# Attention and gated feed-forward on one core: value products by two query tiles, and the maxima of two heads in one VectorE instruction

## The chip, the core and the metric

The kernel runs on one core of a Trainium2 chip. The core has a matmul engine (TensorE, PE in the profile), three elementwise engines (VectorE or DVE, ScalarE or ACT, GpSimd or POOL), and SyncE (SP), which here issues the DMAs. The engines have their own instruction streams and wait for each other with semaphores. The metric is the device time of one execution in microseconds; the median of the runs is compared.

## The reference

Two layers act on x of 4 x 512 x 512. Each adds to x an attention of the normalised x, multiplied by a gate that a feed-forward network makes of the same normalised x. The change touches layer 0 only:

```
xn   = layernorm(x)
q    = xn @ Wq   (32 heads of 16);   k, v = xn @ Wk, xn @ Wv   (8 heads of 16, each shared by 4 query heads)
p    = softmax(q k^T / 4)            (512 x 512 for each head and batch)
s    = concat(p v) @ Wo
g    = silu(down(fwht(silu(gate(fwht(xn))) * up(fwht(xn)))))   (512 -> 2048 -> 512, fwht is a Walsh-Hadamard transform)
x    = x + s * g
```

Layer 1 (a delta-rule attention over six heads and a feed-forward network with sign weights) follows. It is not touched.

## The kernel before, in words

Layer 0's work is written out by hand as a list of steps t from 0 to 295. Every engine runs its own loop over t and, in each step, does whatever is due at that t. Nothing is planned at run time: an engine's instructions go in the order of its loop, and semaphores make it wait for the others.

A unit u is one batch with one key head and its four query heads: 32 units of 8 steps, so a batch is 64 steps. In a unit, two steps belong to one query tile of 128 rows; these two are called a double step here. In it:

- `scores` (TensorE, even step): four matmuls of 32 x 128 by 32 x 512, one for each of the four heads, side by side in the array, into four PSUM banks (the first two banks are the tensor `vpair`). It waits until the four exponentials of the tile before are done, since these read the same banks.
- `row_max` (VectorE, even step): four reduces of 128 x 512, one for each head, negated.
- `exps` (ScalarE): the exponentials of heads 0 and 1 in the even step, of heads 2 and 3 in the odd one, written as fp16 to one of three slots of `probs`.
- `turn_probs` (SP, next even step): a DMA transpose of the four heads' probabilities to a quarter of the columns of `probsT`. From the second unit on it waits for the value products of the unit before (L344).
- `weigh` (TensorE, third step of the next unit): the value products of the whole unit, 16 matmuls of 128 x 32 by 128 x 512 over four column tiles, into the bank `OB`. It stands behind the scores of that step and waits for all four transposes.
- `to_tokens`, `divide`, `to_features` (VectorE, some of the divisions on POOL): a transpose of `OB`, the division by the sum of the exponentials, and the transpose back, at steps 3, 4 and 6 of the next unit.
- `load_heads` (SP, step 6): eight small DMAs that spread k and q of the unit after the next over the partitions.

Beside the attention run the feed-forward products. In the last 32 steps of a batch (m from 32 on) TensorE does a gate tile in the even step and an up tile in the odd one, eight matmuls of 512 columns each (`ffn_mm`), into two banks in turn. ScalarE makes tanh of the gate tile (`tanh_gate`, odd step, ahead of the exponentials), VectorE multiplies (`gate_mul`, `up_mul`), ScalarE copies the result to fp16 (`high_rows`, at the end of the even step, between the two pairs of exponentials), POOL or VectorE makes the rest (`low_rows`). A matmul into a bank waits until the tile two before has been taken from it. In the first 32 steps of the next batch (m below 32) TensorE does the down products, six matmuls in each step (`down_mm`). I call these stretches gate stage and down stage. In the first batch the first 32 steps hold instead the Hadamard transform of the up and gate weights: POOL's and VectorE's sums, fp32 matmuls (`transform_ug`), and copies by ScalarE (`high_half`, after the exponentials) and VectorE (`low_half`). From step 49 the down weights are transformed likewise. The projections of q, k and v of later units lie at steps 5 of every 16, and 43 and 49 of the batch; their evictions by ScalarE follow one step later. The output projection lies in steps 17, 19, 28 and 35.

In TensorE's loop of a step the order is: scores, value products, transposes of x, weight transforms, sums, and then the feed-forward products.

## Time and profile before

| | us |
|---|---|
| median of 3 runs | 1487.92 (1484.96 to 1489.2) |
| profiled execution | 1479.72 |
| its span, first to last instruction | 1477.9 |
| TensorE busy | 1278.4 (87%) |
| VectorE busy | 1058.7 (72%) |
| ScalarE busy | 775.1 (52%) |
| POOL busy | 524.5 (35%) |
| mean granted TensorE clock | 0.963 |

The shares are means over the whole span. Layer 0's steps end at about 840 us and the rest is layer 1, where TensorE is busy nearly all the time; in layer 0 it is not. Busy time of TensorE counts matmuls with their whole pipeline, whose ends are modelled. The granted clock is 1.0 at 2.4 GHz.

### The profile page before, as it was taken

The page shows a single profiled execution, that of the slowest core. Times are in us where ns is not written, and L with a number is a line of the kernel's source. Part 1 is how long each engine was busy: PE and PEld are TensorE (multiplying, and loading weights), DVE is VectorE, ACT ScalarE, POOL GpSimd, SP SyncE. Part 2 cuts the span into 40 slices and gives each one's busy share as a digit, 9 for nine tenths or more (in the row PEclk, how much of TensorE's full clock was granted, in tenths as well). Part 3 has the DMA queues.
Part 4 walks back from the last instruction along what each step waited for, and adds up shares of the span by engine and source line. Part 5 has one row for each costly group of instructions (what it writes and reads, how often), then busy time and mean ns, then how long its engine had stood idle before and what let it go on. Part 6 is the DMA issues. An engine that isn't in the chain of part 4 may idle for free. (4 is left out here: it accounts for less than half of the span.)

```text
span 1477.9 us, 22423 instructions
## 1 busy us (share of the span) xinstructions
PE 1278.4 (87%) x8226; PEld 640.0 (43%) x8226; DVE 1058.7 (72%) x1823; ACT 775.1 (52%) x1308; POOL 524.5 (35%) x434
## 2 busy tenths in 40 slices
PE   4777788777877787877888899999999999999998
PEld 2232333232322233322333355585548654765466
DVE  6688877666766567656777498687878688669846
ACT  5676666554655557545661775236533554246532
POOL 2389853002210022100221156323733274317531
PEclk9899999998999999999999999999999999999999
DMA  7775545565555665565657502300230111210221
GB/s 242 187 168 99 92 91 90 105 123 104 92 104 98 130 114 98 106 119 114 112 102 227 212 20 55 86 16 29 55 71 23 37 45 43 55 37 19 55 48 44
DMA packets 346557, 135.52 MB, mean 92 GB/s; under 512 B 312176, under 2 KB 333392, under 8 KB 343888
## 3 DMA queue, kind: packets, MB, share of 16 engines
q1 hardware_dynamic: 334032, 132.52, 40.6%
q10 hardware_dynamic: 12416, 1.57, 1.0%
q8 instruction: 66, 1.08, 0.3%
q14 instruction: 43, 0.35, 0.1%
HBM read 44.87 MB, written 17.87 MB: 42 GB/s over the span
## 5 line engine op out<-in xcount | busy, mean ns | idle before, releaser
L929 ACT ACTIVATE probs<-vpair,top_n 128x512 f16<-128x512 f32 x256 | 164.4, 687 | 256.3 <-DVE top_n L627 256.3
L1143 PE MATMUL bank<-rows,both 128*128 128x512 f16 x1024 | 244.7, 392 | 5.2 <-DVE fd L700 4.1
L627 DVE TENSOR_REDUCE top_n<-vpair 128x1 f32<-128x512 f32 x256 | 164.5, 684 | 84.9 <-PE bank L1114 82.8
L443 POOL TENSOR_TENSOR h<-th,h 128x512 f16<-128x512 f32 x61 | 71.5, 1172 | 271.5 <-ACT h L898 271.5
L627 DVE TENSOR_REDUCE top_n<-bank 128x1 f32<-128x512 f32 x256 | 163.7, 681 | 0.0
L929 ACT ACTIVATE probs<-bank,top_n 128x512 f16<-128x512 f32 x256 | 162.6, 690 | 0.0
L1143 PEld LDWEIGHTS bank<-rows,both 128*128 128x128 f16 x1024 | 97.5, 100 | 144.5 <-issue 35.4
L2218 PE MATMUL bank<-rows,both 128*128 128x512 f16 x512 | 118.3, 382 | 0.0
L1114 PE MATMUL vpair<-qk 32*128 32x512 f16 x256 | 50.4, 389 | 74.4 <-ACT probs L929 74.4
L2234 PE MATMUL bank<-both,hid 128*128 128x512 f16 x512 | 111.2, 379 | 0.0
L1128 PE MATMUL bank<-probsT,vaug 128*32 128x512 f16 x512 | 45.3, 487 | 72.3 <-DMA probsT<-probs 60.4
L1157 PE MATMUL bank<-dn,h 128*128 128x512 f16 x256 | 104.1, 407 | 0.9 <-DVE tg L633 0.9
L2202 PE MATMUL bank<-rows,both 128*128 128x512 f16 (+1 forms) x456 | 104.0, 379 | 0.9 <-PEq L159 0.9
L1158 PE MATMUL bank<-dn,h 128*128 128x512 f16 x256 | 103.1, 403 | 0.0
L1159 PE MATMUL bank<-dn,h 128*128 128x512 f16 x256 | 102.4, 400 | 0.0
L633 DVE SCALAR_TENSOR_TENSOR tg<-tg,bank 128x512 f32<-128x512 f32 x64 | 44.0, 687 | 72.3 <-ACT tg L941 71.8
L456 POOL TENSOR_TENSOR otok<-oblk,rl 128x256 f16<-128x256 f32 x25 | 15.5, 620 | 180.0 <-DVE rl L673 180.0
L2234 PEld LDWEIGHTS bank<-both,hid 128*128 128x128 f16 x512 | 50.1, 98 | 60.4
L2218 PEld LDWEIGHTS bank<-rows,both 128*128 128x128 f16 x512 | 48.4, 100 | 55.4 <-issue 0.8
L1114 PEld LDWEIGHTS vpair<-qk 32*128 32x128 f16 x256 | 12.9, 91 | 131.3 <-ACT probs L929 74.2
L2202 PEld LDWEIGHTS bank<-rows,both 128*128 128x128 f16 (+1 forms) x456 | 43.6, 98 | 55.5 <-issue 4.4
L1593 POOL TENSOR_TENSOR big<-big,both 128x384 f32<-128x384 f32 x32 | 32.0, 1026 | 94.5 <-DMA big<-t_scratch 70.3
(362 smaller groups left out, 2673.3 us busy)
## 6 DMA issues: line engine op xcount, KB each, us to landing
h<-in_ug SPq DMA_DIRECT2D x8, 1024.0 KB, 5.8
lt_scratch<-big SPq DMA_DIRECT2D x16, 384.0 KB, 2.7
dn<-in_down SPq DMA_DIRECT2D x2, 2048.0 KB, 11.1
x_scratch<-th SPq DMA_DIRECT2D x16, 256.0 KB, 2.6
res<-x_scratch SPq DMA_DIRECT2D x16, 256.0 KB, 4.1
out_x<-res SPq DMA_DIRECT2D x16, 256.0 KB, 2.0
both<-in_w SPq DMA_DIRECT2D x2, 1548.0 KB, 11.9
t_scratch<-tok SPq DMA_DIRECT2D x16, 192.0 KB, 2.1
```

The costliest lines, as they stand in the source:

```text
L443: pool.tensor_tensor(h16(ft, 1), row32, h16(ft, 0), ALU.subtract).then_inc(S["row_lo"], 1)
L627: v.tensor_reduce(top_n[:, i:i + 1], SC_[n % G][:, :], AX.X, ALU.max, negate=True).then_inc(S["max_done"], 1)
L929: a.activation(probs[:, k % TAKEN, j * T:(j + 1) * T], SC_[j][:, :], ACT.Exp, bias=top_n[:, i:i + 1]).then_inc(S["p_ready"], 1)
L1114: pe.matmul(SC_[j][:, :], qs[32 * j:32 * j + 32, u % SLOTS, qt * P:(qt + 1) * P], ks[32 * j:32 * j + 32, u % SLOTS, :], start=True, stop=T ...
L1128: mm = pe.matmul(OB[32 * j:32 * j + 32, :], vaug[:, b % 2, kt, g, :], probsT[:, TT * j + kt, :], start=kt == 0, stop=kt == TT - 1)
L1143: mm = pe.matmul(GB[n % 2][:, :], w[:, kt, col:col + P], xnb(b, kt), start=r == 0, stop=r == 2 * KT - 1)
L1157: pe.matmul(bk, h16(ft, 0)[:, rows], dn16(ft, 0), start=j == 0, stop=False)
L1158: pe.matmul(bk, h16(ft, 0)[:, rows], dn16(ft, 1), start=False, stop=False)
L1159: mm = pe.matmul(bk, h16(ft, 1)[:, rows], dn16(ft, 0), start=False, stop=j == FT - 1)
L2202: mm = pe.matmul(bk, lhs(i, kt), rhs(j, kt), start=n == 0, stop=n == 3 * KT - 1)
L2218: mm = pe.matmul(fbank[ht % 2][:, :], up[:, kt, ht * P:(ht + 1) * P], x_half(i, kt), start=kt == 0 and i == 0, stop=kt == KT - 1 and i == 1)
L2234: mm = pe.matmul(fbank[tt % 2][:, :], hid[:, i, ht, tt * P:(tt + 1) * P], down[:, ht, :], start=ht == 0 and i == 0, stop=ht == HT - 1 and ...
```

## The change

The value products of a unit are made in two halves of two query tiles each (256 columns), two double steps after the last exponentials that they need; a transpose waits only for the half product that read its place. Token transposes, divisions and feature transposes move to later steps. The maxima of heads 0 and 1 come from one reduce over both banks of `vpair`; those of heads 2 and 3 stay single. TensorE does some feed-forward matmuls of a double step (four or three of the gate tile, one or none of the down products) ahead of the scores, and transposes of x and the weight transforms too. ScalarE copies `high_rows` and `high_half` ahead of the step's exponentials. The head loads are split into k (step 6) and q (step 2 of the unit before), and the evictions of q, k and v come two steps after their projection from step 70 on. Semaphore counts of `pv_done` double everywhere.

```diff
@@ -32,7 +32,9 @@
 BSTEPS = NKV * STEPS
 SLOTS = 4
 TAKEN = 3
-PV_STEP, TOKEN_STEP, DIVIDE_STEP, TURN_BACK = 2, 3, 4, 6
+TOKEN_STEP, DIVIDE_STEP, TURN_BACK = 4, 6, 2
+GATE_AHEAD, DOWN_AHEAD = (4, 3), (1, 0)
+LATE_EVICT = 70
 OT = KT + 1
 FFN_STEP = 32
 DOWN_END = (8, 16, 24, 32)
...
@@ -307,7 +309,13 @@
                     sp.wait_ge(S["s_ps"], (u - SLOTS + 1) * SC)
                 for j in range(G):
                     sp.dma_start(ks[32 * j:32 * j + DH, slot, :], kst[DH * g:DH * g + DH, :]).then_inc(S[f"heads_in{slot}"], 16)
+
+            def load_q(u):
+
+                slot = u % SLOTS
                 sp.wait_ge(S["mb_took"], MB["q", u // 2] + 1)
+                if u >= SLOTS:
+                    sp.wait_ge(S["s_ps"], (u - SLOTS + 1) * SC)
                 for j in range(G):
                     r = 64 * (u % 2) + DH * j
                     sp.dma_start(qs[32 * j:32 * j + DH, slot, :], qst[r:r + DH, u // 2 % 2, :]).then_inc(S[f"heads_in{slot}"], 16)
...
@@ -341,11 +349,12 @@
                 u, qt = divmod(n, TT)
                 sp.wait_ge(S["p_ready"], G * (n + 1))
                 if u:
-                    sp.wait_ge(S["pv_done"], u)
+                    sp.wait_ge(S["pv_done"], n // 2 - 1)
                 sp.dma_start_transpose(probsT[:, :, qt * P:(qt + 1) * P], probs[:, n % TAKEN, :]).then_inc(S[f"pt_in{n % TAKEN}"], 16)
 
-            load_heads(0)
-            load_heads(1)
+            for u in range(2):
+                load_k(u)
+                load_q(u)
             sp.dma_start(wsd[:, :], d["wscale_dp"].partition_broadcast(P)).then_inc(S["wo_in"], 16)
             for t in range(TEND):
                 b, m = t // BSTEPS - 1, t % BSTEPS
@@ -362,8 +371,10 @@
                     sp.dma_start(wo[:, :, :], d["wo"]).then_inc(S["wo_in"], 16)
                 if (t - PREP - 2) % 4 == 0 and 2 <= (t - PREP - 2) // 4 + 2 < NCH:
                     load_chunk((t - PREP - 2) // 4 + 2)
-                if t % STEPS == STEPS - 2 and 1 < t // STEPS + 2 < NU:
-                    load_heads(t // STEPS + 2)
+                if t % STEPS == 6 and t // STEPS + 2 < NU:
+                    load_k(t // STEPS + 2)
+                if t % STEPS == 2 and 1 < t // STEPS + 1 < NU:
+                    load_q(t // STEPS + 1)
                 if b >= 0 and m in XRES_STEP:
                     tt = XRES_STEP.index(m)
                     n = b * TT + tt
...
@@ -620,6 +631,12 @@
             def half_scale():
                 v.tensor_scalar(top[:, 4:5], powr[:, 0:1], 0.5 * float(D) ** -0.5 / SUM_RAISE, None, ALU.mult).then_inc(S["pow_b"], 1)
 
+            def two_maxima(n):
+
+                v.wait_ge(S["s_ps"], n + 2)
+                i = n % (2 * SC)
+                v.tensor_reduce(top_n[:, i:i + 2], W["vpair"][:, :, :], AX.X, ALU.max, negate=True).then_inc(S["max_done"], 2)
+
             def row_max(n):
 
                 v.wait_ge(S["s_ps"], n + 1)
...
@@ -659,7 +676,7 @@
 
             def to_tokens(u):
 
-                v.wait_ge(S["pv_done"], u + 1)
+                v.wait_ge(S["pv_done"], 2 * (u + 1))
                 if u:
                     v.wait_ge(S["o_done"], u)
                 v.transpose(oblk[:, :, :].rearrange("p c d -> p (c d)"), OB[:, :]).then_inc(S["o_free"], 1)
@@ -790,8 +807,9 @@
                 if t > FFN_STEP + 1 and (t - 2) // BSTEPS < B and (t - 2) % BSTEPS >= FFN_STEP and t % 2 == 0:
                     up_mul((t - 2) // BSTEPS, ((t - 2) % BSTEPS - FFN_STEP) // 2)
                 if t < NU * STEPS and t % 2 == 0:
-                    for j in range(G):
-                        row_max(2 * t + j)
+                    two_maxima(2 * t)
+                    row_max(2 * t + 2)
+                    row_max(2 * t + 3)
                 if t == 1:
                     statistics(3)
                 if t == 2:
@@ -812,8 +830,8 @@
                     to_tokens(t // STEPS - 1)
                 if t % STEPS == DIVIDE_STEP and 0 <= t // STEPS - 1 < NU:
                     divide(t // STEPS - 1)
-                if t % STEPS == TURN_BACK and 0 <= t // STEPS - 1 < NU and t // STEPS % 2 == 0:
-                    to_features(t // STEPS - 1)
+                if t % STEPS == TURN_BACK and 0 <= t // STEPS - 2 < NU and t // STEPS % 2:
+                    to_features(t // STEPS - 2)
                 if b == B and m == 3:
                     next_stats()
                     weight_max(0)
...
@@ -980,28 +998,29 @@
                     deviations(3)
                 if t == 3:
                     normalise(3)
+                if t > FFN_STEP + 1 and (t - 2) // BSTEPS < B and (t - 2) % BSTEPS >= FFN_STEP and t % 2 == 0:
+                    high_rows((t - 2) // BSTEPS, ((t - 2) % BSTEPS - FFN_STEP) // 2)
                 if b < B and m > FFN_STEP and m % 2:
                     tanh_gate(b, (m - FFN_STEP) // 2)
+                if 0 <= t - PREP - 2 < NCH * KT:
+                    high_half(t - PREP - 2)
                 if t < NU * STEPS:
                     exps(2 * t)
                     exps(2 * t + 1)
                 if t in TURN_STEP:
                     evict_x(KT + TURN_STEP.index(t))
-                if 0 <= t - PREP - 2 < NCH * KT:
-                    high_half(t - PREP - 2)
                 for ft in range(FT):
                     if ABS_AT[ft] == t:
                         magnitudes(ft)
                 if t in DN_AT:
                     high_down(DN_AT.index(t))
-                if t % 16 == Q_STEP + 1 and t // 16 + 1 < NU // 2:
+                late = 1 if t < LATE_EVICT else 2
+                if t % 16 == Q_STEP + late and t // 16 + 1 < NU // 2:
                     evict_q(t // 16 + 1)
-                if m == V_STEP + 1 and b + 1 < B:
+                if m == V_STEP + late and b + 1 < B:
                     evict_v(b + 1)
-                if m == K_STEP + 1 and b + 1 < B:
+                if m == K_STEP + late and b + 1 < B:
                     evict_k(b + 1)
-                if t > FFN_STEP + 1 and (t - 2) // BSTEPS < B and (t - 2) % BSTEPS >= FFN_STEP and t % 2 == 0:
-                    high_rows((t - 2) // BSTEPS, ((t - 2) % BSTEPS - FFN_STEP) // 2)
                 if b and m - 1 in DOWN_END:
                     tanh_down((b - 1) * TT + DOWN_END.index(m - 1))
                 if b == B and m == 9:
@@ -1114,18 +1133,20 @@
                     pe.matmul(SC_[j][:, :], qs[32 * j:32 * j + 32, u % SLOTS, qt * P:(qt + 1) * P],
                               ks[32 * j:32 * j + 32, u % SLOTS, :], start=True, stop=True).then_inc(S["s_ps"], 1)
 
-            def weigh(u):
-
+            def weigh(n):
+
+                u, half = divmod(n, 2)
                 b, g = divmod(u, NKV)
-                for i in range(TAKEN):
-                    pe.wait_ge(S[f"pt_in{i}"], 16 * ((TT * (u + 1) - 1 - i) // TAKEN + 1))
-                if u:
+                for k in (2 * n, 2 * n + 1):
+                    pe.wait_ge(S[f"pt_in{k % TAKEN}"], 16 * (k // TAKEN + 1))
+                if u and half == 0:
                     pe.wait_ge(S["o_free"], u)
-                if g == 0:
+                if g == 0 and half == 0:
                     pe.wait_ge(S["mb_took"], MB["v", b] + 1)
+                cols = slice(2 * P * half, 2 * P * (half + 1))
                 for kt in range(TT):
                     for j in range(G):
-                        mm = pe.matmul(OB[32 * j:32 * j + 32, :], vaug[:, b % 2, kt, g, :], probsT[:, TT * j + kt, :],
+                        mm = pe.matmul(OB[32 * j:32 * j + 32, cols], vaug[:, b % 2, kt, g, :], probsT[:, TT * j + kt, cols],
                                        start=kt == 0, stop=kt == TT - 1)
                 mm.then_inc(S["pv_done"], 1)
 
...
@@ -1144,21 +1165,29 @@
                 if r == 2 * KT - 1:
                     mm.then_inc(S["gb_full"], 1)
 
-            def down_mm(n, j):
+            def down_mm(n, j, r):
 
                 k, ft = GO["down", n], DN_TURN[j]
-                if j == 0:
+                if j == 0 and r == 0:
                     pe.wait_ge(S["gb_took"], k - 1)
-                if n % TT == 0:
+                if n % TT == 0 and r == 0:
                     pe.wait_ge(S["row_lo"], n // TT * FT + ft + 1)
-                if n == 0:
+                if n == 0 and r == 0:
                     pe.wait_ge(S["mb_took"], MB["dn", j] + 1)
                 bk, rows = GB[k % 2][:, :], slice(n % TT * P, (n % TT + 1) * P)
-                pe.matmul(bk, h16(ft, 0)[:, rows], dn16(ft, 0), start=j == 0, stop=False)
-                pe.matmul(bk, h16(ft, 0)[:, rows], dn16(ft, 1), start=False, stop=False)
-                mm = pe.matmul(bk, h16(ft, 1)[:, rows], dn16(ft, 0), start=False, stop=j == FT - 1)
-                if j == FT - 1:
+                mm = pe.matmul(bk, h16(ft, r // 2)[:, rows], dn16(ft, r % 2), start=j == 0 and r == 0, stop=j == FT - 1 and r == 2)
+                if j == FT - 1 and r == 2:
                     mm.then_inc(S["gb_full"], 1)
+
+            def ffn(t, first, last):
+
+                b, m = t // BSTEPS, t % BSTEPS
+                if b and m < FFN_STEP:
+                    for i in range(first, min(last, 6)):
+                        down_mm((b - 1) * TT + m // 8, 2 * (m % 8) + i // 3, i % 3)
+                if b < B and m >= FFN_STEP:
+                    for r in range(first, last):
+                        ffn_mm(b, m - FFN_STEP, r)
 
             def turn_next():
                 pe.wait_ge(S["p_ready"], NU * SC)
@@ -1194,24 +1223,23 @@
             sum_maxima(0)
             for t in range(TEND):
                 b, m = t // BSTEPS, t % BSTEPS
-                if t < NU * STEPS and t % 2 == 0:
-                    scores(t // 2)
-                if t % STEPS == PV_STEP and 0 <= t // STEPS - 1 < NU:
-                    weigh(t // STEPS - 1)
                 if t in TURN_STEP:
                     turn_x(KT + TURN_STEP.index(t))
                 if 0 <= t - PREP - 2 < NCH * KT:
                     transform_ug(t - PREP - 2)
+                ahead = 0
+                if t % 2 == 0:
+                    ahead = (DOWN_AHEAD if m < FFN_STEP else GATE_AHEAD)[t // 2 % 2]
+                ffn(t, 0, ahead)
+                if t < NU * STEPS and t % 2 == 0:
+                    scores(t // 2)
+                if t % 4 == 0 and 0 <= t // 4 - 2 < 2 * NU:
+                    weigh(t // 4 - 2)
+                ffn(t, ahead, 2 * KT)
                 if t > 0 and t % 4 == (PREP + 1) % 4 and (t - PREP) // 4 < NCH:
                     sum_maxima((t - PREP) // 4)
                 if t in DN_AT:
                     transform_dn(DN_AT.index(t))
-                for half in range(2):
-                    if b and m < FFN_STEP:
-                        down_mm((b - 1) * TT + m // 8, 2 * (m % 8) + half)
-                    if b < B and m >= FFN_STEP:
-                        for r in range(KT * half, KT * half + KT):
-                            ffn_mm(b, m - FFN_STEP, r)
                 if t % 16 == Q_STEP and t // 16 + 1 < NU // 2:
                     project_q(t // 16 + 1)
                 if m == V_STEP and b + 1 < B:
```

## Rows read from the trace of the kernel before

**Rows 1.** Busy time by stretch; then TensorE's granted clock, DMA share, GB/s.
```profile
21.44:242.90 221.46, 170.18 (x747) 67.37 (x747) 171.20 (x283) 152.26 (x261) 147.93 (x112) 0.95 0.60 130
242.90:777.48 534.58, 417.92 (x2233) 160.88 (x2233) 354.11 (x575) 302.78 (x505) 82.56 (x82) 0.93 0.59 108
242.90:327.95 85.05, 67.67 (x350) 25.36 (x349) 53.42 (x88) 45.20 (x74) 7.00 (x8) 0.92 0.62 117
427.19:513.53 86.34, 64.11 (x341) 23.88 (x341) 50.21 (x84) 42.86 (x70) 7.01 (x8) 0.90 0.59 116
605.47:690.20 84.73, 63.81 (x340) 23.87 (x341) 50.22 (x84) 42.86 (x70) 7.01 (x8) 0.92 0.63 118
88.00:170.00 82.00, 61.80 (x272) 24.02 (x273) 70.17 (x117) 53.27 (x95) 78.71 (x62) 0.96 0.60 119
461.00:472.00 11.00, 9.72 (x52) 4.00 (x52) 8.21 (x14) 7.32 (x12) 0.62 (x1) 1.00 0.56 106
```

**Rows 2.** Timeline of a double step in a gate stage: start, length, engine, line.
```profile
422.36 0.39 PE L1114 MATMUL vpair<-qk 32*128 32x512 f16 x2 [1.04 <-ACT probs L929]
...
422.69 3.63 PE L1143 MATMUL bank<-rows,both 128*128 128x512 f16 x16
422.78 1.29 DVE L627 TENSOR_REDUCE top_n<-vpair 128x1 f32<-128x512 f32 x2
423.51 1.29 ACT L929 ACTIVATE probs<-vpair,top_n 128x512 f16<-128x512 f32 x2 [1.20 <-DVE top_n L627]
...
424.69 0.62 ACT L898 ACTIVATE h<-th 128x512 f16<-128x512 f32 x1
425.21 0.68 ACT L941 ACTIVATE tg<-bank,usc 128x512 f32<-128x512 f32 x1
...
425.78 1.26 ACT L929 ACTIVATE probs<-bank,top_n 128x512 f16<-128x512 f32 x2
425.92 0.69 DVE L633 SCALAR_TENSOR_TENSOR tg<-tg,bank 128x512 f32<-128x512 f32 x1 [0.65 <-ACT tg L941]
...
427.19 0.39 PE L1114 MATMUL vpair<-qk 32*128 32x512 f16 x2 [0.87 <-ACT probs L929]
```

**Rows 3.** Timeline of a double step in a down stage; last, one single reduce.
```profile
461.05 0.39 PE L1114 MATMUL vpair<-qk 32*128 32x512 f16 x2
...
461.47 1.29 DVE L627 TENSOR_REDUCE top_n<-vpair 128x1 f32<-128x512 f32 x2 [3.50 <-PE bank L1114]
...
464.74 0.39 PE L1114 MATMUL vpair<-qk 32*128 32x512 f16 x2 [0.59 <-ACT probs L929]
...
L627 DVE TENSOR_REDUCE top_n<-vpair 128x1 f32<-128x512 f32 x256 | 164.5, 684 | 84.9 <-PE bank L1114 82.8
```

**Rows 4.** Timeline at value products in a gate stage.
```profile
410.90 1.05 PE L1128 MATMUL bank<-probsT,vaug 128*32 128x512 f16 x16 [1.57 <-DMA probsT<-probs]
...
411.88 5.28 PE L1143 MATMUL bank<-rows,both 128*128 128x512 f16 x16
```

**Rows 5.** Timeline at value products in a down stage, with SP's issues.
```profile
466.59 2.99 SPq L309 DMA_DIRECT2D qk<-kst  x4
...
467.08 1.29 ACT L929 ACTIVATE probs<-bank,top_n 128x512 f16<-128x512 f32 x2
...
469.63 2.48 SPq L313 DMA_DIRECT2D qk<-qst  x4
...
472.21 1.80 SPq L345 DMA_TRANSPOSE probsT<-probs  x1
...
476.81 1.90 PE L1128 MATMUL bank<-probsT,vaug 128*32 128x512 f16 x16 [4.02 <-DMA probsT<-probs]
```

**Rows 6.** Line 1128, the value products: what ended TensorE's idle time before them.
```profile
  DMA probsT<-probs: 91.2, 31
```

**Rows 7.** Lines 345 (transpose, landing) and 561 (a reduce of 2048 elements, ns).
```profile
DMA to landing us min/median/max: 4.3/4.3/10.7
...
L561 DVE TENSOR_REDUCE amax<-h x7: 2252/2274/2277, 33.3 to 120.3; 128x1 f32<-128x2048 f32 x7
```

**Rows 8.** Timeline, first gate stage: VectorE waits for POOL.
```profile
147.64 0.75 DVE L646 SCALAR_TENSOR_TENSOR th<-bank,hsc,tg 128x512 f32<-128x512 f32 x1 [3.29 <-POOL hsc L429]
```

More of the change, by code:

```diff
@@ L298, in _, with load_k @@
             load_chunk(1)
-            def load_heads(u):
+            def load_k(u):
                 b, g, slot = u // NKV, u % NKV, u % SLOTS
@@ L330, in load_raw @@
                 if i == 0:
-                    sp.wait_ge(S["pv_done"], NU)
+                    sp.wait_ge(S["pv_done"], 2 * NU)
                 if i == 2:
@@ L917, in evict_v @@
                 if b >= 2:
-                    a.wait_ge(S["pv_done"], (b - 1) * NKV)
+                    a.wait_ge(S["pv_done"], 2 * (b - 1) * NKV)
                 a.activation(vaug[:, b % 2, :, :, 0:DH], MISC[:, :].rearrange("p (t g c) -> p t g c", t=TT, g=NKV),
```

## Prediction

> **What bounds the kernel now.** I read the stretches first. Layer 0's attention runs from 21.44 to 777.48 us, 128 double steps of one query tile each; the rest, 700.4 us of the span, the diff hardly touches. The first batch's stage takes 221.46 us for 32 double steps, the three stages with down products 85.05, 86.34 and 84.73 (16 double steps each), and the three with up and gate products what is left of 534.58, that is 278.5 for 47 intervals [rows 1]. No engine is full in them: TensorE is busy 64 of 86 us, ScalarE 43, VectorE 50. So a ring of waits sets the pace, and the timeline shows it. In a gate stage: scores at 422.36, first maximum 0.42 later, first exponential at 423.51, two exponentials until the row copy at 424.69, tanh at 425.21, the last two exponentials from 425.78 to 427.04, next scores at 427.19. Round trip 4.83; TensorE's 16 products of 3.63 lie inside, with idle time behind them [rows 2]. In a down stage it is 3.69 [rows 3].
>
> Once in four double steps the value products break this ring. In the gate stage they wait 1.57 us for a transpose, and the 16 products behind them then take 5.28 instead of 3.63, at half clock (1.2 of 2.4 GHz: their pitch doubles) [rows 2, 4]. In the down stage it is worse. The exponentials of the last tile end at 468.4, but SP is still issuing the head loads (2.99 + 2.48 us), its transpose goes out only at 472.21 and TensorE's wait of 4.02 ends at 476.81, 8.4 after the data was ready [rows 5]. The matmul's own line sums 91.2 us of TensorE idle for this DMA, 31 times [rows 6].
>
> **The change, part by part**, against the profiled execution's 1479.72 us (span 1477.9 and 1.8 around it).
>
> *Value products by two query tiles, later.* The last transpose a half needs is issued after its own double step, and the product stands behind two further rounds: 2 x 4.2 = 8.4 us at the least, against 4.3 from issue to landing [rows 7]. That covers landing even with one head load (3.0) ahead of it on SP. I take the wait as gone, and with it the half clock behind it. The matmuls double in number and halve in columns: two groups of 16 in place of one that holds TensorE for 0.98 [rows 4]. Each new group costs between 0.5 (half the columns) and 0.98 (as before); I take 0.8. In a down double step TensorE then has 0.33 for the scores, 0.8, and 12 products at a pitch of 0.216 ((3.63 - 0.39) / 15, [rows 2]), 3.7, in a gate one, with 16, 4.6, both below the rings computed next, so it costs nothing; without that cover it would be 0.6 per unit, 19 us.
>
> *One maximum over two banks.* One 128x512 reduce lasts 0.68, one of 2048 elements 2.27 [rows 3, 7]: 1.04 ns an element, so 1024 take 1.22 (at most 1.29, the pair's time). VectorE saves 0.07, but the first exponential now waits 1.22 instead of 0.68: +0.54 on the ring in every double step. This is the change's price. On the pair, the second reduce is already issued before the first ends (1.29 for two, 0.68 for one), so little start cost is exposed. The Trainium skill (Advanced Engine Details and Errata, TRN2 Errata) says the memory latency shows as a bubble between instructions and recommends reading several PSUM banks at once. By that rule merging would save VectorE more; the sum would not move, since VectorE does not bind here.
>
> *The down ring.* 3.69 + 0.54 = 4.23. Nothing else of the change lies in it (the products put ahead of the scores run while TensorE would wait for exponentials). 48 x 4.23 = 203, plus 4 for double steps in which the output projection (1.03) meets value products: 207 against 256.1, so -49.
>
> *The gate ring.* The row copy (0.52 from start to start) moves ahead of the exponentials, into the time in which ScalarE waits for the maximum: it leaves the ring. But three or four gate products now stand ahead of the scores, and the bank of each gate needs the previous gate's multiply on VectorE. Counted from the scores: maximum 0.42 to 1.64, exponential at 1.69, tanh 1.18 later at 2.87, ends 3.55, multiply 3.58 to 4.27, 0.12 of semaphore, then 4 or 3 products at 0.216: scores again at 5.25 or 5.04, mean 5.14 [rows 2]. The exponentials alone would allow 3.44 + 1.26 + 0.15 = 4.85, so the wait for the multiply takes the place of the wait for exponentials. 47 x 5.14 = 242, plus 3 for projections: 245 against 278.5, so -34.
>
> *Token transposes and division, one or two steps later; transpose of features in the next unit.* Same instructions. The token transpose (0.7) now falls between the last maximum (2.9) and the multiply (3.58), which it just fits; if it doesn't, 0.1 per unit, 3 us at most. Lost cover: nothing waits for it within two rounds.
>
> *Head loads split, late q, k and v evictions.* SP issues the same eight loads of a unit, at most 3.0 us in one block rather than 5.5 [rows 5]. The evictions move off the middle of the ring to behind it; that frees about 0.5 sixteen times, inside the totals above. load_q gains a wait on scores that are over by then; behind it on SP stands the next transpose, and behind that the exponentials three tiles on and the value products two rounds on, so a microsecond here reaches nobody. The k eviction of a next batch now comes one step after the last q load it waits for (2.5 on SP and its landing); ScalarE stands still for at most 2 us, three times, behind exponentials that are already done.
>
> *First batch.* POOL is busy 78.7 of 82 us between 88 and 170, with weight transforms that gate what follows [rows 1], and up_mul waits 3.29 for it [rows 8]. So at most 3 there. In the other 139 us I take 9%, under the gate stage's 12% because the fp32 transforms add TensorE and VectorE work: 12. Bounds of the term 0 and 25; I take 15. Moving the weight-transform copy ahead of the exponentials hides it in the wait for the maximum there, which about pays the 0.54.
>
> *Tail.* The last value products lose a 2 us wait; 1.
>
> Sum: 49 + 34 + 15 + 1 = 99. Rings worked out from single rows come out short; the next down round after the 3.69 is 3.77 already (464.74 to 468.51, 0.14 after the exponentials that end in rows 5). I add 0.1 to each of the 95 double steps for it, 9.5. That leaves -90: 1390 profiled. The runs of before have median 1487.92, 8.2 above their profiled one; I carry the difference over: 1398.
>
> **Rivals.**
> A. The multiply isn't late, and the gate ring is 4.85: 47 x 0.29 = 14 less, 1384. For it: each step in 5.14 is a minimum-slack sum, and one overlap would shorten it. Against: bank order is fixed by the code. 0.15.
> B. SP becomes the bound of the down stages. Its work in a unit is 4 transposes at 1.8 and 5.5 of loads [rows 5], 12.7 of 17 us. If an issue took half as long again because the DMA queues are fuller, and the residual's transfers, one or two of a microsecond, came on top, it would be 18 to 19. 12 units x 2 us: 1422. Against: at 4.2 us apart transposes are further from each other than their issue. 0.14.
> C. Half the gate gain and all of the first batch's are eaten by POOL and by products that meet in one double step: 1398 + 17 + 15 = 1430. 0.13.
> D. The clock falls: slower. TensorE would idle 0.4 to 1.2 us in every double step (5.14 or 4.23 less its 3 to 4.6 of work), without end. At half clock a gate double step needs 16 x 0.43 (twice the pitch) + 0.7 = 7.6 instead of 5.14 and a down one 12 x 0.43 + 0.7 = 5.9 instead of 4.23: about 2 us each. If all 95 ran so: 190, 1588; from 45 of them on it is slower than before. Against: between stalls the present ring has the same gaps (0.59 to 1.04) and the granted clock of a stretch with three of them is 1.00 [rows 1 to 3]. The Trainium skill (TensorE: Matmul & The Clock Gate, on a second failure mode) warns of just this, many short idles between groups making the clock oscillate; by that rule this rival would be the case, and the trace so far does not agree. 0.04.
> E. The value products still wait, because a transpose now waits for the product two halves back and the two drift together. Then only the half clock goes: 28 x 1.65 = 46 less, against 48 x 0.54 and 47 x 0.31 more on the rings: 5 less, 1483, within what can be told. 0.04.
> My forecast: 0.50, for itself 1384 to 1412.
>
> **Numbers.** Predicted 1398. The range 1374 to 1432 takes in A, B and C and the term bounds of the first batch (+15, -10) and of the maximum (1.29: +0.07 x 95 = 7). A measurement tells 0.3%, 4.5 us. Faster: forecast, A, B, C and the milder half of E and D, 0.93; same: 0.04; slower: D at its full price, 0.03.
>
> **What would show it.** The value products' idle for the transpose (91.2) falls under 10; the maximum over two banks lasts 1.22; down double steps 4.2, gate ones 5.0 and 5.25 in turn, with TensorE's idle ahead of the gate products put down to the multiply (tg), not to the exponentials; granted clock 1.00 in all six stages; stages of about 70 and 82 us. I am wrong if down double steps exceed 4.6, if the transposes go out later than 1 us after their exponentials, or if half-clock stretches remain.

## The result and the profile after

The changed kernel takes 1432.32 us (median of 4) against 1486.66 for the kernel before: ratio 0.9637, 95% interval 0.9616 to 0.9657. It is 54 us faster; I had said 90 (1398), and the time lies just above the range's upper end, 1432. The profiled execution's span went from 1477.9 to 1430.6.

These are the stretches from one stage's first scores to the next, in the columns of [rows 1]: the start; the first 32 steps; the whole first batch, which contains them; then down and gate stages in turn; the tail.

```profile
0.00:25.39 25.39, 11.84 (x47) 5.57 (x49) 16.17 (x46) 10.33 (x19) 7.52 (x12) 1.00 0.64 213
25.39:160.64 135.25, 92.19 (x359) 35.17 (x360) 90.42 (x142) 85.14 (x145) 86.76 (x62) 0.86 0.64 148
25.39:262.89 237.50, 176.58 (x857) 68.20 (x857) 166.84 (x247) 151.51 (x256) 147.07 (x112) 0.91 0.57 121
...
262.89:338.93 76.04, 62.72 (x417) 25.32 (x417) 52.69 (x73) 44.93 (x75) 6.50 (x8) 1.00 0.72 131
338.93:424.39 85.46, 72.93 (x477) 29.08 (x478) 67.65 (x93) 59.66 (x100) 21.54 (x21) 1.00 0.64 112
424.39:494.94 70.55, 58.95 (x408) 23.96 (x408) 48.78 (x68) 41.94 (x70) 6.50 (x8) 1.00 0.78 142
494.94:580.41 85.47, 72.94 (x477) 29.06 (x478) 67.66 (x93) 59.66 (x100) 21.54 (x21) 1.00 0.64 112
580.41:650.95 70.54, 58.95 (x407) 23.96 (x408) 48.77 (x68) 41.94 (x70) 6.50 (x8) 1.00 0.79 142
650.95:731.49 80.54, 66.82 (x435) 25.91 (x435) 63.83 (x87) 54.78 (x91) 19.77 (x19) 1.00 0.63 110
731.49:1430.60 699.11, 680.63 (x5220) 406.51 (x5219) 516.78 (x922) 313.80 (x530) 287.97 (x229) 0.99 0.23 62
```

Beside [rows 1]: the down stages fell from 256.1 to 217.1 us, the three gate stages from 278.5 to 251.5, and all six now run at clock 1.00 (0.92, 0.90 and 0.92 in the down stages before). The first batch rose from 221.5 to 237.5, and it starts 4 us later; the whole rise lies in its first 32 steps, which in the kernel before took 117.5 us:

```profile
21.44:138.90 117.46, 85.56 (x311) 34.39 (x311) 89.62 (x155) 86.78 (x150) 76.31 (x49) 0.93 0.70 169
```
So 66 us were gained in the six stages, 20 were lost before them, and 1 was gained in the tail.

The value products' wait is gone. The idle time before the line, all of it, was 91.2 us for the DMA [rows 6] and 68.2 of "issue" (the engine waited for nothing that the profile shows); now it is 15.3 of "issue" alone:

```profile
L1149 PE MATMUL bank<-probsT,vaug x1024: 272/273/421, 58.8 to 742.4; 128*32 128x256 f16 x171
its engine sat idle before it (us, times) until:
  issue: 15.3, 64
```

Next a double step of a gate stage, as in [rows 2]: the 12 or 13 products behind the scores, the merged maximum, tanh, the multiply (DVE L650), three products of the next tile ahead of the scores, the next scores.

```profile
403.77 0.39 PE L1133 MATMUL vpair<-qk 32*128 32x512 f16 x2
...
404.09 0.62 PE L1149 MATMUL bank<-probsT,vaug 128*32 128x256 f16 x16
...
404.30 1.23 DVE L638 TENSOR_REDUCE top_n<-vpair 128x2 f32<-128x1024 f32 x1 [0.77 <-PE bank L1133]
404.65 2.76 PE L1164 MATMUL bank<-rows,both 128*128 128x512 f16 x12
405.44 1.28 DVE L644 TENSOR_REDUCE top_n<-bank 128x1 f32<-128x512 f32 x2
405.56 1.27 ACT L947 ACTIVATE probs<-vpair,top_n 128x512 f16<-128x512 f32 x2 [1.36 <-DVE top_n L638]
406.71 0.69 ACT L959 ACTIVATE tg<-bank,usc 128x512 f32<-128x512 f32 x1
407.28 1.27 ACT L947 ACTIVATE probs<-bank,top_n 128x512 f16<-128x512 f32 x2
407.43 0.69 DVE L650 SCALAR_TENSOR_TENSOR tg<-tg,bank 128x512 f32<-128x512 f32 x1 [0.71 <-ACT tg L959]
...
408.18 0.82 PE L1164 MATMUL bank<-rows,both 128*128 128x512 f16 x3 [0.76 <-DVE tg L650]
408.93 0.39 PE L1133 MATMUL vpair<-qk 32*128 32x512 f16 x2
```

The ring of the prediction can be followed step by step: the maximum lasts 1.23, the multiply is over at 408.12, the products that waited for it (`<-DVE tg`) start at 408.18, and the scores at 408.93, 5.16 after the last ones. The first exponential comes 1.79 after the scores; in the kernel before it was 1.15 [rows 2]. The exponentials were over at 408.55, so they no longer set the pace.

In the first 32 steps TensorE transposes x (L1053) ahead of the weight transform (L1074) and the scores (L1133), and a transpose can wait for ScalarE's eviction (L879) of the one before. Here ScalarE ends step 17 and TensorE begins step 18:

```profile
100.86 1.27 ACT L947 ACTIVATE probs<-bank,top_n 128x512 f16<-128x512 f32 x2
...
102.00 0.62 ACT L879 ACTIVATE rows<-bank 128x512 f16<-128x512 f16 x1
...
102.77 0.38 PE L1053 MATMUL bank<-ident,both 128*128 128x128 f16 x4 [2.89 <-ACT rows L879]
102.99 1.08 PE L1074 MATMUL bank<-h,had 128*128 128x512 f32 x2
...
104.86 0.39 PE L1133 MATMUL vpair<-qk 32*128 32x512 f16 x2
104.96 0.69 ACT L897 ACTIVATE both<-bank,suc 128x512 f16<-128x512 f32 x1 [1.82 <-PE bank L1075]
```

The exponentials end at 102.13. Scores that waited for them alone could have come at about 102.25 (an estimate: 0.12 for the semaphore, as in the prediction). They come at 104.86, since an eviction, a transpose and a transform stand in between.

### The profile page after: what moved, and what is told of

It is laid out like the page before. It is cut to its first block and busy times, and to the rows that moved or that the text cites. A ratio compares the mean times of both kernels' runs of the same rounds, so it can differ in the third digit from the quotient of the medians.

```text
span 1430.6 us, 23477 instructions
## 1 busy us (share of the span) xinstructions
PE 1262.4 (88%) x8738; PEld 637.6 (45%) x8738; DVE 1049.2 (73%) x1695; ACT 778.5 (54%) x1308; POOL 524.9 (37%) x434
## 3 DMA queue, kind: packets, MB, share of 16 engines
q8 instruction: 70, 1.15, 0.4%
## 5 line engine op out<-in xcount | busy, mean ns | idle before, releaser
L638 DVE TENSOR_REDUCE top_n<-vpair 128x2 f32<-128x1024 f32 x128 | 156.7, 1224 | 129.2 <-PE bank L1133 129.2
L1178 PE MATMUL bank<-dn,h 128*128 128x512 f16 x768 | 179.0, 382 | 5.9 <-DVE tg L650 3.3
L1164 PEld LDWEIGHTS bank<-rows,both 128*128 128x128 f16 x1024 | 90.7, 98 | 182.9 <-DVE tg L650 63.0
L1178 PEld LDWEIGHTS bank<-dn,h 128*128 128x128 f16 x768 | 71.3, 98 | 99.0 <-issue 14.6
L1133 PE MATMUL vpair<-qk 32*128 32x512 f16 x256 | 50.8, 392 | 30.2 <-ACT probs L947 29.9
L2246 PEld LDWEIGHTS bank<-rows,both 128*128 128x128 f16 x512 | 48.5, 100 | 55.9 <-issue 1.7
L650 DVE SCALAR_TENSOR_TENSOR tg<-tg,bank 128x512 f32<-128x512 f32 x64 | 43.9, 686 | 25.2 <-ACT tg L959 22.8
L916 ACT ACTIVATE h<-th 128x512 f16<-128x512 f32 x64 | 40.4, 631 | 37.2 <-DVE th L663 37.2
L1575 POOL TENSOR_TENSOR hid<-sil 128x512 f32<-128x512 f32 x24 | 33.1, 1380 | 62.4 <-DVE sil L1695 62.4
L1133 PEld LDWEIGHTS vpair<-qk 32*128 32x128 f16 x256 | 12.5, 91 | 97.2 <-issue 51.1
```

What stands on the lines that cost most here:

```text
L638: v.tensor_reduce(top_n[:, i:i + 2], W["vpair"][:, :, :], AX.X, ALU.max, negate=True).then_inc(S["max_done"], 2)
L650: v.scalar_tensor_tensor(tg[:, :], tg[:, :], 1.0, GB[n % 2][:, :], ALU.add, ALU.mult).then_inc(S["gb_took"], 1)
L916: a.activation(h16(ft, 0), row32, ACT.Copy).then_inc(S["row_hi"], 1)
L1133: pe.matmul(SC_[j][:, :], qs[32 * j:32 * j + 32, u % SLOTS, qt * P:(qt + 1) * P], ks[32 * j:32 * j + 32, u % SLOTS, :], start=True, stop=T ...
L1164: mm = pe.matmul(GB[n % 2][:, :], w[:, kt, col:col + P], xnb(b, kt), start=r == 0, stop=r == 2 * KT - 1)
L1178: mm = pe.matmul(bk, h16(ft, r // 2)[:, rows], dn16(ft, r % 2), start=j == 0 and r == 0, stop=j == FT - 1 and r == 2)
```

## The experiments

Each ratio is against the kernel before, timed beside that version. The ratios' intervals are 0.002 to 0.004 to either side. The changed kernel was not timed again beside them, and the kernel before had medians of 1481.8 to 1482.8 there, some 4 us under the 1486.66 above. So differences to the changed kernel, which I take from the medians, can be 4 to 5 us too favourable; where it matters the difference by the ratios stands beside them. "Stage" times are from the profiled execution, first scores to first scores.

**1. The scores and value products ahead again in the first 32 steps (TensorE's order).**
```diff
-                if t in TURN_STEP:
-                    turn_x(KT + TURN_STEP.index(t))
-                if 0 <= t - PREP - 2 < NCH * KT:
-                    transform_ug(t - PREP - 2)
                 ahead = 0
...
                     weigh(t // 4 - 2)
+                if t in TURN_STEP:
+                    turn_x(KT + TURN_STEP.index(t))
+                if 0 <= t - PREP - 2 < NCH * KT:
+                    transform_ug(t - PREP - 2)
                 ffn(t, ahead, 2 * KT)
```


> The changed kernel with one thing undone: in the first 32 steps TensorE again does the scores and value products of a step ahead of the transposes of x and of the up/gate weight transforms (it still does the feed-forward products ahead of the scores later on). Theory 1, the order on TensorE: in the first batch the scores stand behind a transpose that waits for an eviction by ScalarE and behind 1.9 us of fp32 transforms, so the ring of a double step is lengthened; the stage from the first scores to the first down stage (237.5 us after, 221.5 before) falls to 205 to 215 and the whole by 22 to 32 us, to about 1405. Theory 2, the order on ScalarE (the weight copy waits for the transform ahead of the exponentials): little changes here, 5 us at most. Theory 3, neither, but the later or doubled value products or head loads: no change.

1435.08, ratio 0.9679 (0.9656 to 0.9702): nothing gained. The first 32 steps took 142.3 us. Theory 1 fails in this form. The trace shows why: now ScalarE's weight copy (L897), which still stands ahead of the exponentials, waits for a transform that stands behind the scores. Between 25 and 140 us these waits sum to 44.4 us, against 27.4 in the changed kernel:

```profile
ACT both L897 <- PE bank L1075: 44.4, 15, 4.5
```

**2. Exponentials ahead of the weight copy again (ScalarE's order).**
```diff
-                if 0 <= t - PREP - 2 < NCH * KT:
-                    high_half(t - PREP - 2)
                 if t < NU * STEPS:
                     exps(2 * t)
                     exps(2 * t + 1)
                 if t in TURN_STEP:
                     evict_x(KT + TURN_STEP.index(t))
+                if 0 <= t - PREP - 2 < NCH * KT:
+                    high_half(t - PREP - 2)
```


> The changed kernel with one thing undone: in the first 32 steps ScalarE again does the exponentials and the eviction of x ahead of the copy of the transformed weights (high_half). Theory 1 (TensorE's order): at most 8 us faster than the changed kernel, since the scores still come late. Theory 2 (ScalarE's order): 20 us or more faster, 1412 or less. Theory 3: no change.

1432.74, ratio 0.9667: nothing either, 136.4 us for the first 32 steps. The copy's wait all but vanishes (2.6 us), but the transposes of x wait for ScalarE's eviction as before; first this version between 25 and 140 us, then the changed kernel:

```profile
PE bank L1053 <- ACT rows L879: 23.1, 7, 4.2
PE bank L1053 <- ACT rows L879: 21.8, 7, 4.6
```

**3. Both**, that is the two diffs above together.

> The changed kernel with both orders of the first 32 steps undone, on TensorE and on ScalarE. My term for the first batch in the prediction (15 us faster than before, a stage of 206 us) should appear here if the orders alone made the error: total 1397, 35 us below the changed kernel. Theory 3 (the value products in halves, the late loads, or POOL make the first batch slow): within 5 us of the changed kernel, 1427 or more. Also tells whether the two add up or one is enough.

1416.73, ratio 0.9554: 16 us below the changed kernel (12 by the ratios), under half of the 35 I expected. The first 32 steps took 123.2 us and started 3.7 earlier. So the two orders belong together: with TensorE's alone undone, ScalarE waits to copy what TensorE has not made yet; with ScalarE's alone undone, TensorE waits for a bank that ScalarE has not read yet.

**4. Only the 12 transposes of x behind the scores again.**
```diff
-                if t in TURN_STEP:
-                    turn_x(KT + TURN_STEP.index(t))
                 if 0 <= t - PREP - 2 < NCH * KT:
                     transform_ug(t - PREP - 2)
...
                     weigh(t // 4 - 2)
+                if t in TURN_STEP:
+                    turn_x(KT + TURN_STEP.index(t))
                 ffn(t, ahead, 2 * KT)
```

> The changed kernel with only the transposes of x (12 of them in the first 26 steps) put back behind scores and value products on TensorE; the weight transforms stay ahead. It splits theory 1: if the transposes, which wait for ScalarE's eviction of the one before, are the cause, this takes 15 us or more off the changed kernel (1417 or less); if it is the transforms' own time and their waits for VectorE's copies, 5 us or less.

1415.34, ratio 0.9550 (0.9526 to 0.9573), 17 us below the changed kernel (13 by the ratios). This one edit alone gives as much as experiment 3. The first 32 steps, and the rest of the first batch:

```profile
24.68:142.29 117.61, 89.19 (x359) 33.77 (x360) 89.73 (x142) 84.33 (x145) 85.48 (x61) 0.89 0.72 171
142.29:248.15 105.86, 88.89 (x498) 33.88 (x498) 76.72 (x105) 66.48 (x111) 61.78 (x52) 0.94 0.46 81
```
The first 32 steps fall from 135.3 to 117.6 with the same instructions on the engines (POOL has one fewer in the stretch).

**5. The evictions first on ScalarE, the transposes still ahead on TensorE.**
```diff
+                if t in TURN_STEP:
+                    evict_x(KT + TURN_STEP.index(t))
                 if 0 <= t - PREP - 2 < NCH * KT:
                     high_half(t - PREP - 2)
                 if t < NU * STEPS:
                     exps(2 * t)
                     exps(2 * t + 1)
-                if t in TURN_STEP:
-                    evict_x(KT + TURN_STEP.index(t))
```


> The changed kernel with ScalarE's evictions of the transposed x (12, in the first 26 steps) moved ahead of the step's weight copy and exponentials; TensorE keeps the transposes ahead of the scores. turn_back took 17 us off. Theory 1a, the wait: a transpose ahead of the scores waits for the eviction of the one before, which stands behind two exponentials on ScalarE; then this edit frees the same wait from the other side and takes 12 us or more off (1420 or less). Theory 1b, the mere place of the transpose and of the sum of maxima behind it in the common bank: 4 us or less.

1413.37, ratio 0.9536 (0.9506 to 0.9565), 19 us below the changed kernel (15 by the ratios); first 32 steps 114.5 us. The transpose ahead of the scores does no harm that these times show once its eviction does not stand behind two exponentials: TensorE's idle time before L1053 for the eviction is 22.1 us in the changed kernel and 8.1 here.

```profile
25.02:139.51 114.49, 85.48 (x359) 32.72 (x360) 91.72 (x142) 83.90 (x145) 85.18 (x61) 0.90 0.73 175
```

**6. No gate products ahead of the scores.**
```diff
-GATE_AHEAD, DOWN_AHEAD = (4, 3), (1, 0)
+GATE_AHEAD, DOWN_AHEAD = (0, 0), (1, 0)
```


> The changed kernel with no gate products ahead of the scores (the down stages keep theirs). My step in the prediction says that in the gate stages the scores stand behind four or three products that wait for VectorE's multiply (tg), and that the exponentials alone would allow 4.85 to 4.95. Then gate double steps fall from 5.16 and 5.38 to 4.9, the three gate stages from 251.5 to about 233, the whole by 15 to 18 us to about 1416; TensorE's wait for tg vanishes and its wait for the exponentials comes back. Rival: the products ahead only fill time, and the value products plus 16 products behind the scores make TensorE late instead: no change or slower, gate double steps with value products at 5.3 or more.

1410.55, ratio 0.9530 (0.9491 to 0.9568): 22 us below the changed kernel by the medians, 16 by the ratios. The gate stages fall to 80.1, 80.1 and 74.2 us, 17.0 less together, inside the expectation of 15 to 18. Most double steps are 4.82 to 4.93, with and without value products (the others 5.1 to 5.5), and the exponentials release the scores again:

```profile
401.62 0.39 PE L1133 MATMUL vpair<-qk 32*128 32x512 f16 x2 [0.98 <-ACT probs L947]
401.95 0.62 PE L1149 MATMUL bank<-probsT,vaug 128*32 128x256 f16 x16
402.50 3.63 PE L1164 MATMUL bank<-rows,both 128*128 128x512 f16 x16
406.45 0.39 PE L1133 MATMUL vpair<-qk 32*128 32x512 f16 x2 [0.32 <-ACT probs L947]
```

**7. Four single maxima.**
```diff
-                    two_maxima(2 * t)
-                    row_max(2 * t + 2)
-                    row_max(2 * t + 3)
+                    for j in range(G):
+                        row_max(2 * t + j)
```


> The changed kernel with four single maxima in place of the one over two banks and two single ones. If the merged maximum lengthens every ring by 0.54 us as predicted, down double steps fall from 4.26 to 3.72, gate ones from 5.27 to 4.73 on the mean, and the whole by 50 to 60 us, to 1372 to 1382. Rival 1: at 3.7 us the transposes (DMA engines busy 0.78 of the down stages at 4.26) or SP's issues bind, and a down double step does not go below 4.0: 1395 or more. Rival 2: the single maxima cost VectorE its 0.07 us per double step and the ring is bound elsewhere: no change.

1389.18, ratio 0.9379 (0.9348 to 0.9411): 43 us below the changed kernel (38 by the ratios), the largest term. Steady down double steps fall from 4.25 to 3.67, and neither the transposes nor SP bind at that pace. Here are two scores of the timeline and, in the columns of [rows 1], the stretch behind them, with the DMA engines at 0.78:

```profile
411.19 0.39 PE L1132 MATMUL vpair<-qk 32*128 32x512 f16 x2 [0.24 <-ACT probs L946]
414.87 0.39 PE L1132 MATMUL vpair<-qk 32*128 32x512 f16 x2 [0.38 <-ACT probs L946]
```
```profile
411.19:418.00 6.81, 6.43 (x48) 2.79 (x49) 5.19 (x9) 4.46 (x8) 0.00 (x0) 1.00 0.78 159
```
It is less than 50, since the gate stages give only 5 each (80.5 for 85.5): in a steady unit of theirs the double steps take 4.5 to 5.1, with the products ahead and the value products both in the way. Without the products ahead (the second version of experiment 10) these stages take 77.3 and 76.1 us, so they are about 4 us of it; the part of the value products was not tested.

**8. The merged maximum alone, in the kernel before.**
```diff
-                    for j in range(G):
-                        row_max(2 * t + j)
+                    two_maxima(2 * t)
+                    row_max(2 * t + 2)
+                    row_max(2 * t + 3)
```

> The kernel before with one part of the change done alone: the maxima of heads 0 and 1 by one instruction over two banks. Theory (ring): its 0.54 us is added to every double step that the exponentials bind, 128 at most: 40 to 65 us slower than before, 1525 to 1550, with down double steps at 4.2 in place of 3.7. Rival: the stall at the value products and the first batch's other waits absorb it: under 20 us slower. Rival 2: saving 0.07 us of VectorE per double step makes it faster by up to 9 us.

1496.79, ratio 1.0108 (1.0072 to 1.0144): 14 us slower, well under the ring theory's 40 and in line with the rival that the stall absorbs it. The maximum lasts 1.225 there too, and down double steps without value products are 4.26. But the longer ring gives the transposes more time, and the stall it was added to shrinks: the value products' idle time for the DMA fell from 91.2 us to

```profile
  DMA probsT<-probs: 63.2, 31
```
The three gate stages take 278.5 us together, as before. So its price depends on what else stands still: 14 us beside the stall, about 40 once the stall is gone.

**9. The split of the head loads alone, in the kernel before.**
```diff
-                if t % STEPS == STEPS - 2 and 1 < t // STEPS + 2 < NU:
-                    load_heads(t // STEPS + 2)
+                if t % STEPS == 6 and t // STEPS + 2 < NU:
+                    load_k(t // STEPS + 2)
+                if t % STEPS == 2 and 1 < t // STEPS + 1 < NU:
+                    load_q(t // STEPS + 1)
```


> The kernel before with one part of the change alone: the head loads of k at step 6 for the unit after the next and of q at step 2 for the next unit, in place of all eight at step 6. My reading of rows 5: SP's 5.5 us of loads hold up the last transpose of a unit by 3.7 us in the down stages, and with it the value products. Then a down double step with value products falls from 8.8 to 10.5 us by 2 to 3 us, a gate one by 1 to 2, and the whole by 35 to 65 us, to 1420 to 1450. Rival: the transposes' own 4.3 us to land and their wait for the value products before (L344) make the stall: under 12 us.

1434.52, ratio 0.9682 (0.9647 to 0.9716): 47 us faster by the order in which SP issues a unit's eight small DMAs. The down stages take 76.2, 76.6 and 74.9 us, and the wait for the DMA falls to 38.4. In the unit shown the last transpose goes out 1.7 us after its exponentials, which end at 450.4, and not 3.8 as in [rows 5]; the value products wait 1.81 and not 4.02, and run at full clock (1.05 us for the longest group, not 1.90):

```profile
449.24 2.82 SPq L309 DMA_DIRECT2D qk<-kst  x4
450.59 0.39 PE L1123 MATMUL vpair<-qk 32*128 32x512 f16 x2 [0.68 <-ACT probs L938]
452.16 1.78 SPq L351 DMA_TRANSPOSE probsT<-probs  x1
...
456.69 1.05 PE L1137 MATMUL bank<-probsT,vaug 128*32 128x512 f16 x16 [1.81 <-DMA probsT<-probs]
```

**10. What the runs point to.** These are three versions without the terms that lose, all with the single maxima of experiment 7. The first has no feed-forward products ahead of the scores and both orders of experiment 3:
```diff
-GATE_AHEAD, DOWN_AHEAD = (4, 3), (1, 0)
+GATE_AHEAD, DOWN_AHEAD = (0, 0), (0, 0)
```

> The changed kernel with the merged maximum, the feed-forward products ahead of the scores, and the orders of the first 32 steps undone; what is left of the change is the value products in halves two double steps later, the later token steps, the split head loads, the later evictions and the earlier row copy. By the terms measured so far: down double steps 3.7, gate ones 4.5 to 4.6 where value products make TensorE the bound and 4.4 elsewhere, first batch 15 to 20 us under the changed kernel: 1340 to 1365. Rival: the transposes or SP bind below 4.2 us per double step: 1390 or more.

1359.13, ratio 0.9178 (0.9140 to 0.9215). The second has no gate products ahead, as in experiment 6, and the transposes of experiment 4, the third no gate products ahead either and the evictions of experiment 5 (their diffs, nothing else).

> A version that the runs point to: the changed kernel with single maxima, no gate products ahead of the scores, and the transposes of x behind the scores; weight transforms and weight copies stay ahead. By the terms measured (17 for the transposes, 43 for the maxima, 17 for the gate products) it should be near 1355; if the orders of the first 32 steps are better as in halves_only, a few us above its 1359, otherwise below.

1357.90, ratio 0.9161 (0.9133 to 0.9189).

> The last candidate: the changed kernel with single maxima, no gate products ahead of the scores, and the evictions of the transposed x ahead of the exponentials. evict_first's first 32 steps took 114.5 us against turn_back's 117.6, all else equal. If the terms add up it is within 3 us of turn_single_gate0 (1358), 1353 to 1360; if the eviction ahead of an exponential that is no longer late costs something, up to 1365.

1353.10 (5 runs), ratio 0.9126 (0.9098 to 0.9154): 79 us below the changed kernel (76 by the ratios). Its first batch takes 203.8 us, for 237.5 in the changed kernel and 221.5 in the one before, at clock 0.97:

```profile
24.86:228.63 203.77, 163.60 (x857) 65.97 (x857) 169.54 (x279) 151.36 (x256) 147.25 (x112) 0.97 0.65 141
228.63:651.12 422.49, 388.07 (x2617) 160.42 (x2617) 350.11 (x575) 308.92 (x506) 82.22 (x82) 1.00 0.74 137
```
The first of the three differs from experiment 9's kernel (1434.52) by the value products in halves with their later token steps, the later evictions and the row copy ahead. Together these are worth 75 us; which gives how much was not run.

## Why the prediction was right and wrong

*The value products' wait* (predicted gone): gone, and all half clock in the six stages with it. Each half of 16 matmuls holds TensorE for 0.55 to 0.56 (404.09 to 404.65), not 0.8; it costs nothing, as said. Rival D is out (clock 1.00), E too (no wait for the DMA), and so is B: SP keeps up even at 3.67 us a double step in experiment 7.

*The maximum*, 1.22 predicted: 1.225, and 0.54 on the ring: 0.58 (3.67 to 4.25). Both were right within 0.04, and experiments 7 and 8 show them from both sides. That its price is larger in the new kernel than in the old one I had not said.

*The down ring*, 4.23 predicted: 4.25, then 4.35 at the last of a unit. The term was 49 less 4.8 of the allowance, 44; 39.0 was measured. What lies between is, in the main, the two double steps of a batch with output projections (5.39 and 5.17, 2.0 over the ring together, where I had 1.3) and the first down stage, which is 5.5 us longer than the other two.

*The gate ring*, 5.04 and 5.25 predicted, 0.1 of allowance on top: 5.16 and 5.38. (The products start 0.06 behind the multiply, where I had 0.12, and no row showed that.) Experiment 6 shows the cause named, the wait for the multiply; rival A is out. The term was 34 less 4.7, 29; 27.0 was measured. The products ahead of the scores are a loss of 17 us, since without them the stages are that much shorter.

*Head loads*: my reading of rows 5 was right (experiment 9), but I gave the split no price of its own. It is worth nearly as much alone (47 us) as the whole change (54), and it alone takes the wait for the DMA from 91.2 to 38.4 us, which I had put down to the halving.

*The first batch*: here the prediction failed. I wrote that moving the weight copy ahead "about pays the 0.54" and put the term at 15 us of gain, between 0 and 25. It lost 16, and 4 more before the first scores, which now stand behind the first weight transform (behind the scores again, in experiments 1 and 3, they start 3.5 us earlier): an error of 35 of the 43 us between forecast and profiled gain. The step that failed: the paragraph prices ScalarE's copy alone. That TensorE takes the transposes of x and the transforms ahead of the scores, it puts at nothing and gives no reason. I had priced what moves into a wait and not the wait that moves along. A transpose of x waits for the eviction of the one before; put ahead of the scores, it ties them to an eviction that ScalarE does behind its exponentials.

Experiment 4 ends the first batch 14.7 us earlier (248.2 for 262.9), experiment 5 17.5. Their first 32 steps take 117.6 and 114.5 us, so this wait explains the whole rise from the kernel before's 117.5. Part of it is clock: in the first 32 steps it was 0.93 in the kernel before, 0.86 in the changed one, 0.89 and 0.90 in these two; how much of the loss that makes was not taken apart. The maxima are some 6 more (257.3 in experiment 7), little above the spread told below. Nor did moving the copy pay: experiments 3 and 4 differ only in the copy and the transforms, behind in one and ahead in the other, and in time by 1.4 us, where 0.54 in 16 double steps would be 9. The rest, some 12 to 15 us, lies in my guess of 9% for the remainder, which had no row under it, and no run shows what makes it; single maxima and no products ahead bring the first batch to what I had forecast (203.8 against 206), with the evictions first. Experiments 1 and 2 show that undoing one order alone gains nothing, each for another wait: the copy's for the transform in the first, the transpose's for the eviction in the second. The first 32 steps of three kernels that differ only later, or by the maxima (the changed kernel and experiments 6 and 7), took 133 to 141 us, so differences below some 5 us in this part are not read from single profiles.

*Rival C and the signs.* Rival C forecast 1430, 2 us from the result, but not by what happened: it had half of the gate gain lost and the first batch's at nothing, and the gate gain was nearly all there while the first batch went 20 us the other way. That its number fits is luck. Of my signs of being wrong, down double steps above 4.6 appeared at the output projections, at the start of the first down stage and nowhere else, and of the attention's stages only the first batch still ran below clock 1.00. They looked at single double steps of the six stages; none put a number to the first batch, where the error was.

## What to carry to other kernels

When work is moved ahead of the instruction that starts a ring, price what it waits for as part of the ring, not only its own time; moved work that waits for an engine further round makes the ring longer even if there was idle time to fill. Merging two short operations that a consumer takes one by one saves a little of the producer's time (here 0.07 us of VectorE) and costs the consumer the wait for both (here 0.58 in each round). And where one engine issues the DMAs in program order, look first at what it issues ahead of the late transfer: here a mere reordering gave 3%.

## What the runs showed of the hardware

The merged reduce over two PSUM banks takes 1225 ns for 1024 elements against 684 for 512 in one: 541 ns for the second bank. Four column tiles of 32 with 256 columns each take 0.55 us for 16 matmuls, 0.98 with 512 columns [rows 4]. And short idle gaps of TensorE, 0.8 to 1.1 us in most double steps and 1.7 at the longest, for 470 us on end, left the granted clock at 1.00; in the kernel before, the clock of the six stages fell below 1.00 only in double steps with a stall at the value products. The Trainium skill (TensorE: Matmul & The Clock Gate, on a second failure mode) reports a kernel in which frequent short idles between groups of matmuls made the clock swing; no run here showed it in these stages.
